# Two 64x128 mask products a group of scores, in place of eight 64x32 ones

## The reference

```
sim = einsum('bhwie,bhwje->bhwij', bq, bk2) * 8.0      # 8 windows of 32 queries, 64 keys each
sim = where((i < j) | (i > j + 32) | (j == -1), -max, sim)
attn = softmax(sim, -1)
out = einsum('bhwij,bhwje->bhwie', attn, bv2)
```

## Time and profile before

| | us |
|---|---|
| median of 3 runs | 1776.3 (1773.92 to 1778.2) |
| the profiled execution, its own time | 1778.04 |
| its span | 1776.2 |
| PE busy | 1688.0 (95%) |
| DVE busy | 1556.0 (88%) |
| POOL busy | 1426.1 (80%) |
| ACT busy | 1253.0 (71%) |

### The profile page before, as it was taken

The page is one execution under the profiler, slowest core; times in us unless marked ns, Lnnn a source line. Parts: engine busy times, 40 slices in busy tenths (PEclk is TensorE's granted clock), DMA queues, the critical chain, the costliest instruction groups (busy, mean ns, idle before and its releaser), DMA issues.

```text
span 1776.2 us, 73872 instructions
## 1 busy us (share of the span) xinstructions
PE 1688.0 (95%) x30944; PEld 981.9 (55%) x30944; DVE 1556.0 (88%) x2724; ACT 1253.0 (71%) x2325; POOL 1426.1 (80%) x1264
## 2 busy tenths in 40 slices
PE   3789999999999999999999999999999999999986
PEld 1355555555555555555555555555555555555552
DVE  5768999889989899889998899988998989988976
ACT  3566686767876777767778668677687677776764
POOL 1667888987889887988879888898788888788872
PEclk9899999999999999999999999999999999999998
DMA  3013233141312422133321313314131242212340
GB/s 113 22 40 71 51 84 81 40 95 41 82 40 53 106 66 55 30 71 80 82 65 34 79 43 86 84 37 93 42 84 38 53 107 65 55 31 57 75 94 24
DMA packets 94054, 113.13 MB, mean 64 GB/s; under 512 B 42318, under 2 KB 59484, under 8 KB 93724
## 3 DMA queue, kind: packets, MB, share of 16 engines
q1 hardware_dynamic: 93724, 108.41, 25.9%
HBM read 19.22 MB, written 1.05 MB: 11 GB/s over the span
## 4 chain that ended last, share of the span: by engine, by line
PE 61%; DVE 15%; POOL 10%; issue 8%; ACT 3%; SPq 1%; DMA 1%; POOLq 0%; DVEq 0%; ACTq 0%
PE bank L630 12%; PE bank L714 8%; PE bank L655 8%; PE bank L646 6%; PE bank L731 6%; PE bank L675 5%; PE bank L692 4%; DVE qn L1321 3%; PE bank L759 3%; DVE qc L1321 3%; POOL AB L1609 2%; POOL AB L1598 2%; POOL hb L1643 2%; DVE ssq L1328 2%; PE bank L774 2%
## 5 line engine op out<-in xcount | busy, mean ns | idle before, releaser
L1598 POOL TENSOR_TENSOR AB<-qc,qn 128x512 f32<-128x512 f32 x384 | 486.9, 1273 | 105.4 <-DVE qn L1321 103.3
L1609 POOL TENSOR_TENSOR AB<-AB,rinv 128x512 f32<-128x512 f32 x384 | 411.5, 1095 | 34.7 <-DVE rinv L1344 34.7
L630 PE MATMUL bank<-wqkv,XT 128*128 128x512 f32 x768 | 382.2, 600 | 4.6 <-DVE qn L1321 4.5
L1616 POOL TENSOR_TENSOR Pb<-Pb,p_rden 128x512 f32<-128x512 f32 x192 | 200.4, 1044 | 134.4 <-DVE p_rden L1365 132.1
L1004 ACT ACTIVATE qkT<-bank 128x512 f32<-128x512 f32 x384 | 228.9, 596 | 109.3 <-PE bank L655 107.6
L995 ACT ACTIVATE sq<-bank 128x512 f32<-128x512 f32 x384 | 228.4, 595 | 96.1 <-PE bank L630 96.0
L1328 DVE TENSOR_REDUCE ssq<-sq 128x8 f32<-128x512 f32 x384 | 258.4, 673 | 10.2 <-ACT sq L995 9.5
L1321 DVE TENSOR_TENSOR qc<-bank,rt 128x512 f32<-128x512 f32 x384 | 258.6, 673 | 8.8 <-ACT sq L995 5.9
L1321 DVE TENSOR_TENSOR qn<-bank,rt 128x512 f32<-128x512 f32 x384 | 261.5, 681 | 0.0
L714 PEld LDWEIGHTS bank<-PT,V 64*64 64x64 f32 x12288 | 197.0, 134 | 95.3 <-issue 89.2
L655 PE MATMUL bank<-ident,AB 128*128 128x128 f32 x1536 | 243.1, 281 | 4.5 <-ACT qkT L1004 3.3
(11 more groups left out here) (145 smaller groups left out, 2523.0 us busy)
## 6 DMA issues: line engine op xcount, KB each, us to landing
V<-V SPq DMA_DIRECT2D x672, 64.0 KB
rep<-du SPq DMA_DIRECT2D x64, 512.0 KB, 4.7
wqkv<-in_Wqkv SPq DMA_DIRECT2D x36, 256.0 KB, 3.4
XV<-XT SPq DMA_DIRECT2D x96, 64.0 KB, 2.2
wo<-in_Wo SPq DMA_DIRECT2D x6, 512.0 KB, 5.4
BC<-BC SPq DMA_DIRECT2D x8, 256.0 KB
w<-in_W SPq DMA_DIRECT2D x6, 341.0 KB, 4.5
BC<-BC SPq DMA_DIRECT2D x8, 128.0 KB
```

Source lines behind the costliest of these rows:

```text
L630: pe.matmul(R[u % 2][:], XT[:, s % NB, (u % 2) * P:(u % 2 + 1) * P], wqkv[:, (u // 2) * 512:(u // 2 + 1) * 512], start=True, stop=True).th ...
L1598: pool.tensor_tensor(AB[:, n % NAB, :], qc[:, u % 2, :], qn[:, u % 2, :], ALU.add).then_inc(rs_done, 1)
L1609: pool.tensor_tensor(o, o, r, ALU.mult).then_inc(nm_done, 1)
```

## The change

`maskrow` (128 x 128, bf16) takes the place of `identb`. Its columns 32w to 32w+31 hold, in each half of 64 rows, the identity that picks the mask rows of window w. With it one product of 64 rows, 128 output rows and 256 columns writes the mask for a whole half, so a group has two mask products, one in the upper and one in the lower 64 rows of the array, each over all 128 columns. The products of q and k after them are as before. At the start DVE clears `maskrow`, waits for that, and makes eight copies of 32 x 32 in place of one of 128 x 128.

```diff
-        identb = m.sb("identb", [P, P], BF16)
+        maskrow = m.sb("maskrow", [P, P], BF16)
...
                 x_free("scores", g, s)
-                for w in range(4):
-                    for odd in range(2):
-                        p0 = DH * odd
-                        c0 = p0 + (WIN if w else 0)
-                        pe.matmul(SB[w * WIN:(w + 1) * WIN, odd, 0:SEQ], identb[p0:p0 + DH, c0:c0 + WIN],
-                                  maskb[p0:p0 + DH, :], start=True, stop=False, skip_group_check=True)
+                for odd in range(2):
+                    r = slice(DH * odd, DH * (odd + 1))
+                    pe.matmul(SB[:, odd, 0:SEQ], maskrow[r, :], maskb[r, :], start=True, stop=False, skip_group_check=True)
...
             dve.tensor_copy(maskb[:], stage[:]).then_inc(mask_set, 1)
-            dve.tensor_copy(identb[:], ident[:]).then_inc(mask_set, 1)
+            ins = dve.memset(maskrow[:], 0.0)
+            link(ins)
+            for w in range(4):
+                for p0 in (0, DH):
+                    r = slice(p0 + WIN, p0 + DH) if w else slice(p0, p0 + WIN)
+                    ins = dve.tensor_copy(maskrow[r, w * WIN:(w + 1) * WIN], ident[r, r.start:r.stop])
+            ins.then_inc(mask_set, 1)
```

## The result

The changed kernel takes 1791.8 us (median of 5 runs, 1791.13 to 1798.21), the kernel before 1777.34 beside it. The ratio is 1.0086 (95% interval 1.0073 to 1.0098), which is 15.3 us more (13.0 to 17.4). The direction and the range were forecast rightly, the range by 1.8 us at its lower edge of 1790; the forecast size was 23.6.

The account below looks back on a forecast made before the run. PE, busy 95%, was taken as the bound. Terms of +0.14 us a block over 192 blocks gave 26.9 us, 85% of it 22.9, plus 0.7 for the start: 1799.9, stated as 1799, range 1790 to 1814.

Parts of the forecast that it names:

- Term 1: Between mask and scores: one more change of array shape per block, in which nothing starts, +0.10 us.
- term 3: Mask's own weight load, 128 columns in place of 32: +0.04 us a block, 0.02 or less with a fast load.
- the 110 to 140: Sign expected in the profile after: the mask's weight load should take 110 to 140 ns.
- term 2: Mask products: six staggered starts fewer in each block, -0.02 us.
- Term 4: Score weight loads no longer run beneath the mask's stream: +0.02 us a block, at worst +0.09.
- Term 5: Score products: if instruction supply sets the pace, six mask pairs fewer give back 0.06 us; taken as nothing.
- How much reaches the end: Of 192 x 0.14 us, 85% taken to reach the end, 22.9 us; 134 blocks on the chain, 18.8 us, can't be hidden.
- The start: DVE's clear, wait and eight small copies, 1.7 us against 1.05 for one copy: +0.7 us, all on the path.
- Little slower: Instruction supply paces a block's second half, which catches up: +0.02 to +0.06 us a block, 1783.5 us; chance 0.12.
- Faster: No change of shape is seen, score weights load ahead beneath the mask: 1767 us; chance 0.10, including nothing.
- Much slower: The two 64x128 mask products run one after the other, another pass bounded at +0.11 us: 1820 us; chance 0.08.

Follow-up runs that it names:

- e5: Kernel before, PE's wait for the mask weights moved to its first scores, plus one single-column 64x128 product with zero weights between mask and scores: 1815.61 us, ratio 1.0207.
- e9: Changed kernel with the late wait, its two mask products over all 128 rows and 128 columns, lower 64 weight rows zero: 1792.65 us, ratio 1.0084.
- e4: Changed kernel with the late wait, mask written by four products of 64x64 in place of two of 64x128: 1787.11 us, ratio 1.0053.
- e7: Kernel before with the late wait, its eight 64x32 mask products issued twice: 1791.34 us, ratio 1.0073.
- e8: Kernel before with the late wait, mask products taken out, score products starting their sums themselves: 1767.12 us, ratio 0.9944.
- e6: Changed kernel with the late wait, its two 64x128 mask products issued twice: 1799.72 us, ratio 1.0121.
- e10: Kernel before with the late wait, its eight 64x32 mask products issued three times: 1806.71 us, ratio 1.0170.
- e2: Changed kernel, but PE waits for the mask weights only ahead of its first scores: 1790.08 us, ratio 1.0075.
- e1: Changed kernel's start (clear, wait, eight small copies) with the old eight 64x32 mask products: 1777.08 us, ratio 1.0001.
- e3: Kernel before, with PE waiting for the mask weights only ahead of its first scores: 1777.59 us, ratio 0.9997.

## Why the prediction was right, and where its size was off

- **What bounds the kernel.** Right: PE time added in the steady part comes out at the end, PE time taken away comes off, at 38 to 82% of the sum over the blocks.
- **Term 1, the change of shape.** Right, 0.10 forecast and 0.093 to 0.096 in the steps ahead of a change; e5 adds two of them with one column of work and e9 moves one. The row of L838, a change of columns alone, was the one to trust. The Trainium skill's rule on changing the tiling mode ("TensorEngine Tiling (Array Packing)", Key Properties) holds here in the very case that the trace before lacked: 64x128 to 64x32.
- **Terms 2 and 3.** Together they were put at +0.02, and the first score product, 0.093 later than before, leaves nothing for them. The error is mostly in term 3, for which I had taken the f32 rows: the load of 128 bf16 columns takes 92 ns, 3 more than that of 32, not 40, and lies outside the 110 to 140 that I named as a sign. Whether term 2's 0.02 was given back and the load took it, no run separates. The Trainium skill's rule on the fast weight load ("TensorE: Matmul & The Clock Gate", Weight-path perf modes) was the better guide, and e4 agrees with it: at 64 columns the load takes 103 ns, longer than at 128.
- **Term 4, the head start.** Right: 0.02 forecast, 0.016 measured. Block: +0.109 measured, +0.14 forecast.
- **Term 5, pace.** Rightly nothing: e7 and e8 change the number of products by eight and the block by a pass each.
- **How much reaches the end.** This step failed most. I took 85%, a share that no row gave, with 134 blocks on the chain as a floor that can't be hidden. The 134 came from a rounded 5% and one piece of 0.66; counted along the chain of that trace it is 126 (83.1 us of L675). At 0.109 a block a floor of 134 would be 14.6 us, and the kernel after has just that; but e4 lies at 9.4 (at most 11.7) where 134, or 126, times 0.129 says 17 or 16, and e6 at 21.5 where they say 29 or 27. A chain read from one trace didn't bound the effect from below. Nor does it stay: 101 blocks are on it in e8, 136 in the changed kernel, 155 in e10. The part table and the waits show what gave way: PE's waits for L1050 and L1619, and the time right behind the blocks. With the measured block and the 62 to 64% of e2 and e7 the sum is 13.2.
- **The range.** The sum of 1799.9 was set down as 1799; nothing hangs on it. The range's lower edge, 1790, is that floor at 0.10 a block. The time fell 1.8 us inside it, and e4, with the same cause and a longer block, fell below it. That the size of the effect at the end lay inside the range is in part luck.
- **The start.** Forecast 0.7 us, all on the path. DVE's copies made PE start 2.3 us later, three times as much: I had priced a copy at 177 ns, and it takes 358. e1 shows at most 2.1 us of it at the end, and nothing clear of noise. Both halves of the term were off, in opposite directions.
- **The rivals.** "Little slower": e7 and e8 speak against the supply of instructions. "Faster": the first score load stands 0.22 us after the mask, so the change of shape is there. "Much slower": two records span 0.28 us, so the halves run together.

No version that keeps the mask beats the kernel before: e1 and e3 are the same within 0.2%, and all others are slower.

## What to carry to other kernels

Small products in different places of the PE array that run side by side cost one pass: eight of them cost one pass of 0.10 us, sixteen two. Merging the eight bought nothing here, because the merged shape differs from that of the work next to it: a product of another shape costs about 0.10 us and the head start of the loads behind it. In e9 the merged products have the shape of the part ahead, and the time is the same, since the change only moves; no run has a merged shape that equals both neighbours'. So look at the shapes of neighbours in PE's order before counting instructions. And of time added to the engine that bounds this kernel 38 to 82% reached the end, with the other engines busy 70 to 88%; the chain of one trace gave a share, not a floor.

## What the runs showed of the hardware that was not expected

- A bf16 weight load takes 89 ns for 32 columns, 103 for 64 and 92 for 128, in 64 rows.
- The step into another shape is 0.093 to 0.096 us longer than in the same shape, whether the load behind it takes 88 or 135 ns.
- DVE's copy of 32 x 32 elements from f32 to bf16 takes 0.36 us, twice the 177 ns of an instruction on 128 x 16; eight of them cost more than one copy of 128 x 128 (1.05 us), and the copy of 128 x 256 just ahead of them takes only 0.67. The cause was not looked for.
- A product of a single column in another shape lengthened the block by 0.24 us, a pass of 256 columns in the same shape by 0.11.
